# A reordered opening: latents normalised on VectorE, table rows made on GpSimd, third keys ahead of the second half's queries, and expert weights loaded whole

## What is computed

```python
x = x + xattn(layernorm(x), ctx, cos, sin, ...)
x = x + attn(layernorm(x), ...)
x = x + ffn(layernorm(x), ...)
# xattn, b = 8 batches, 16 heads of 64
lat = layer_norm(latents, ln_lat_g, ln_lat_b)
ctx = layer_norm(context, ln_ctx_g, ln_ctx_b)
q = lat @ Wq;  k, v = split(ctx @ Wkv)
k = apply_rope(k, cos, sin)
attn = softmax(clip(q k^T * 64**-0.5, -11, 11));  out = (attn v) @ Wo + bo
# ffn: for the two experts e chosen for a token
out_e = relu(x @ W1[e] + b1[e]) @ W2[e] + b2[e]
```

## Time and profile before

| | |
|---|---|
| median of 3 runs | 1197.59 us (1196.59 to 1199.62) |
| the profiled execution | 1197.26 us, its span 1195.5 us |
| TensorE busy | 1177.0 us (98%) |
| VectorE, ScalarE, GpSimd busy | 1005.6, 649.5, 610.0 us |
| granted TensorE clock | 0.998 over the span |

### The profile page before, as it was taken

How to read it: one execution, slowest core, us unless ns; L and a number is a source line. 1 busy time by engine, 2 the same in 40 slices (tenths; PEclk the granted TensorE clock), 3 DMA queues, 4 the chain that set the end, 5 groups by cost and what they waited for, 6 DMA issues and landing times.

```text
span 1195.5 us, 37336 instructions
## 1 busy us (share of the span) xinstructions
PE 1177.0 (98%) x15252; PEld 992.1 (83%) x15252; DVE 1005.6 (84%) x1923; ACT 649.5 (54%) x1089; POOL 610.0 (51%) x611
## 2 busy tenths in 40 slices
PE   8999999999999999999999999999999999999997
PEld 4787888888888888888888888888888788899997
DVE  7999999999899999999988999998766366768886
ACT  6765555555555555555555555555434243366664
POOL 3576565565655656556666556565452133333333
PEclk9999999999999999999999999999999999999999
DMA  6376665666656665556666566655662721576662
GB/s 239 90 190 155 149 139 145 152 157 161 145 150 151 156 158 145 139 147 151 162 155 151 143 154 155 159 144 121 165 137 72 247 78 58 175 215 207 182 208 57
DMA packets 136180, 181.21 MB, mean 152 GB/s; under 512 B 30332, under 2 KB 96328, under 8 KB 135880
## 3 DMA queue, kind: packets, MB, share of 16 engines
q1 hardware_dynamic: 110552, 150.80, 48.2%
q10 hardware_dynamic: 21376, 23.80, 7.9%
q0 software_dynamic: 4080, 4.22, 1.7%
HBM read 81.93 MB, written 30.56 MB: 94 GB/s over the span
## 4 chain that ended last, share of the span: by engine, by line
PE 89%; DVE 4%; DMA 2%; ACT 2%; issue 1%; SPq 1%; POOL 0%; POOLq 0%; ACTq 0%; DVEq 0%
PE bank L1627 28%; PE bank L1659 28%; PE bank L1600 10%; PE bank L1985 6%; PE bank L1680 3%; PE bank L1789 2%; PE bank L2035 2%; PE bank L2036 2%; PE bank L2037 2%; PE bank L1842 1%; DVE pr L1104 1%; DMA wk_raw<-in_L_xattn_Wkv_dram 1%; PE bank L1885 1%; PE bank L1866 1%; PE bank L1851 1%
## 5 line engine op out<-in xcount | busy, mean ns | idle before, releaser
L1627 PE MATMUL bank<-ct,wk_hi 128*128 128x512 f32 x1024 | 323.5, 397 | 0.7 <-DVE ct L1138 0.7
L1659 PE MATMUL bank<-p_hi,xc 128*128 128x512 f32 x1024 | 316.0, 390 | 0.0
L1659 PEld LDWEIGHTS bank<-p_hi,xc 128*128 128x128 f32 x1024 | 191.8, 188 | 39.7
L1627 PEld LDWEIGHTS bank<-ct,wk_hi 128*128 128x128 f32 x1024 | 187.2, 188 | 41.9 <-issue 1.3
L594 POOL TENSOR_TENSOR kr<-kr,ksw 128x1024 f32<-128x1024 f32 x64 | 153.0, 2391 | 106.9 <-issue 105.5
L1132 DVE TENSOR_TENSOR kw<-bank,stab 128x512 f32<-128x512 f32 x256 | 175.6, 686 | 31.9 <-PE bank L1627 25.3
L1627 PE MATMUL bank<-ct,wk_lo 128*128 128x512 f32 x512 | 200.1, 391 | 0.0
L1659 PE MATMUL bank<-p_lo,xc 128*128 128x512 f32 x512 | 199.2, 389 | 0.0
L790 ACT CAST p_hi<-pr 128x1024 fp32r<-128x1024 f32 x128 | 134.2, 1048 | 89.1 <-DVE pr L1104 88.9
L1104 DVE TENSOR_SCALAR pr<-pr 128x1024 f32<-128x1024 f32 x128 | 137.6, 1075 | 41.5 <-ACT pr L785 39.6
L1120 DVE TENSOR_TENSOR p_lo<-pr,p_hi 128x1024 fp32r<-128x1024 f32 x128 | 168.9, 1320 | 0.5 <-ACT p_hi L790 0.4
(11 more groups left out here) (231 smaller groups left out, 2062.2 us busy)
## 6 DMA issues: line engine op xcount, KB each, us to landing
ksw<-kw SPq DMA_DIRECT2D x512, 128.0 KB, 2.3
x_turned<-xt SPq DMA_DIRECT2D x120, 128.0 KB, 3.3
ct_read<-x_turned SPq DMA_DIRECT2D x30, 512.0 KB, 4.8
w_two<-in_L_ffn_W_dram SPq DMA_DIRECT2D x15, 1024.0 KB, 5.1
raw<-in_ctx_dram ACTq DMA_DIRECT2D x56, 256.0 KB, 3.8
x_slots<-fill ACTq DMA_DIRECT2D x32, 258.0 KB, 3.8
w_all<-in_L_ffn_W_dram SPq DMA_DIRECT2D x4, 2048.0 KB, 17.0
wo<-in_L_ffn_W_dram SPq DMA_DIRECT2D x7, 1024.0 KB, 4.9
```

Source lines behind the costliest of these rows:

```text
L1627: last = pe.matmul(psK[:, a * 512:(a + 1) * 512], l[:, k, w], ct[:, h % 3, r, k], start=(m == 0), stop=(m == len(parts) - 1))
L1659: last = pe.matmul(psZ[c], xc[:, slot_, l, t, cols], r[:, i, :, t], start=(f == 0 and m == 0), stop=(f == 1 and m == len(parts) - 1), skip ...
```

## The change

Six edits to the opening, and one to the loads of the experts. (1) `latent_scale` on GpSimd keeps only the power; VectorE computes the variance term in one instruction and normalises all latent tiles, where ScalarE did tiles 2 to 7. (2) The eight instructions that fill `crep` go from VectorE to GpSimd, and `crep_done` counts each table. (3) `biases` writes four groups of 32 output partitions by 256 columns where it wrote two by 512, and stands ahead of `queries(5, 0)`. (4) TensorE's order: `queries(0, 0)` ahead of `table(0)`, `turn_context(6)` and `(7)` sooner, `keys(2)` and then `keys(3)` ahead of, or between, the other half's queries. (5) ScalarE and VectorE follow that order. (6) SyncE copies the bias row in four pieces. (7) The weights of group 3 are loaded whole where they were loaded in halves, and `first_weights(4)` stands ahead of `rows_in(4)`.

```diff
@@ SyncE
-            sp.wait_ge(bias_done, 1)
-            for i in range(2):
-                sp.dma_start(wv[P - 1:P, KC - 1, i * 512:(i + 1) * 512], bias_rows[HALF * i:HALF * i + 1, :]).then_inc(bias_ld, 16)
+            sp.wait_ge(bias_done, 2)
+            for i in range(4):
+                sp.dma_start(wv[P - 1:P, KC - 1, i * D:(i + 1) * D], bias_rows[HALF * i:HALF * i + 1, :]).then_inc(bias_ld, 16)
...
-            e = expert_of(sp, EARLY)
-            first_weights_of(e, EARLY, 0)
+            first_weights(EARLY)
             sp.wait_ge(group_done, 4)
             sp.wait_ge(scattered, 16 * TOPK * TT)
             for g in range(1, GROUPS):
...
+                if g + WB < GROUPS:
+                    sp.wait_ge(h_ps, FT // 2 * (g + 1))
+                    first_weights(g + WB)
                 if g == 1:
-                    first_weights_of(e, EARLY, 1)
                     sp.wait_ge(ys_done, 2)
                     sp.wait_ge(no_done, 2)
                     rows_in(4)
-                if g + WB < GROUPS:
-                    sp.wait_ge(h_ps, FT // 2 * (g + 1))
-                    first_weights(g + WB)
@@ GpSimd
+            def table_rows(f):
+                for r in range(4):
+                    o = crep[:, f, :, r * HALF:(r + 1) * HALF]
+                    last = pool.tensor_scalar(o, cs_raw[:, f], -1.0 if f == 1 and r % 2 == 1 else 1.0, None, ALU.mult)
+                last.then_inc(crep_done, 1)
             latent_scale(0)
+            pool.wait_ge(cs_ld, 32)
+            table_rows(0)
+            table_rows(1)
@@ ScalarE (order; -/+ whole calls)
-            latents_normalised(2)
-            latents_normalised(3)
...
+            query_weights_high(0)
+            queries(1, 0)
             table(1)
-            queries(1, 0)
+            queries(2, 0)
+            context_high(0)
             key_weights(0)
+            queries(3, 0)
+            context_high(1)
             key_weights(1)
...
+            context_high(6)
+            context_high(7)
             lat_turned(6)
             lat_turned(7)
@@ VectorE
+            latent_variances(0)
+            latents_normalised(0)
...
+            key_weights(1)
             latent_moments(6)
             latent_moments(7)
+            latent_variances(1)
...
+            latents_normalised(1)
             context_low(4)
@@ TensorE
+            queries(0, 0)
             table(0)
-            queries(0, 0)
+            queries(1, 0)
             table(1)
-            queries(1, 0)
             for g in range(2, 7):
+                if g == 5:
+                    biases()
                 queries(g, 0)
                 turn_context(g - 2)
...
+            turn_context(6)
             keys(1)
             turn_lat(6)
             turn_lat(7)
-            biases()
-            turn_context(6)
+            turn_context(7)
             queries(7, 0)
-            turn_context(7)
+            keys(2)
             queries(0, 1)
             queries(1, 1)
-            keys(2)
+            keys(3)
             queries(2, 1)
-            keys(3)
             queries(3, 1)
```

More of the change, by code:

```diff
@@ L114, in build @@
             w_last = sb("w_last", [P, INNER], F32, first)
-            bias_rows = sb("bias_rows", [DH, 512], F32, first)
+            bias_rows = sb("bias_rows", [P, D], F32, first)
+            sb("between_0", [P, D], F32, first)
             crep = sb("crep", [P, 2, ST, P], F32, first)
@@ L721, in lat_turned @@
                 act.wait_ge(latT_ps, t + 1)
-                for k in range(1 if t < TT // 2 else KC):
+                for k in range(1 if 0 < t < TT // 2 else KC):
                     last = act.activation(latT[:, k, t * P:(t + 1) * P], lat_bank(t, k), ACT.Identity,
@@ L732, in biases @@
                 act.wait_ge(bias_ps, 1)
-                act.copy(bias_rows[:], bank[0:DH, 4, :]).then_inc(bias_done, 1)
+                act.copy(bias_rows[:], bank[:, 4, 0:D]).then_inc(bias_done, 1)
             def sum_out(n, c):
@@ L1048, in latent_moments, with latent_variances, latents_normalised @@
                 dve.bn_aggr(xl_mom[:, t], xl_st6[:, t]).then_inc(xl_stats, 1)
+            def latent_variances(c):
+                t = slice(c * TT // 2, (c + 1) * TT // 2)
+                dve.wait_ge(xl_stats, (c + 1) * TT // 2)
+                dve.tensor_scalar(xl_vpe[:, t], xl_mom[:, t, 1], 1.0 + EPS, EPS * EPS, ALU.mult, ALU.add).then_inc(xl_var, 1)
+            def latents_normalised(c):
+                dve.wait_ge(xl_rstd, c + 1)
+                for t in range(c * TT // 2, (c + 1) * TT // 2):
+                    dve.tensor_scalar(xl[:, t], xl[:, t], xl_mom[:, t, 0:1], xl_rsd[:, t:t + 1], ALU.subtract, ALU.mult).then_inc(xl_norm, 1)
             for t in range(TT // 2):
                 latent_moments(t)
[L1052 to L1060, removed]
-                dve.tensor_scalar(xl[:, t], xl[:, t], xl_mom[:, t, 0:1], xl_rsd[:, t:t + 1], ALU.subtract, ALU.mult).then_inc(xl_norm, 1)
+            latent_variances(0)
+            latents_normalised(0)
             dve.wait_ge(vec_done, 1)
-            for u in range(TT // 2):
+            for u in range(1, TT // 2):
                 dve.wait_ge(latT_ps, u + 1)
@@ L1204, in _ @@
             context_low(5)
-            keys_turned(-3, 0)
-            keys_turned(-3, 1)
-            for u in range(TT // 2):
-                latents_low(u)
-            query_weights_low(0)
-            shifts(-3)
-            counted(-3)
-            context_low(6)
             dve.wait_ge(bias_ps, 1)
@@ L1215, in _ @@
             value_weights(0)
-            value_weights(1)
-            context_low(7)
+            keys_turned(-3, 0)
+            keys_turned(-3, 1)
+            context_low(6)
+            shifts(-3)
+            counted(-3)
+            context_low(7)
+            query_weights_low(0)
+            for u in range(TT // 2):
+                latents_low(u)
+            keys_turned(-2, 0)
+            keys_turned(-2, 1)
+            query_weights_low(1)
             blocks_turned(-3)
-            query_weights_low(1)
             shifts(-2)
@@ L1571, in turn_lat @@
             def turn_lat(t):
-                if t < 2:
-                    pe.wait_ge(xl_norm, t + 1)
-                else:
-                    pe.wait_ge(xl_norm_act, t - 1)
+                pe.wait_ge(xl_norm, t + 1)
                 if t == 0:
@@ L1719, in biases @@
                 for k in range(KC):
-                    for c in range(2):
-                        last = pe.matmul(bank[c * HALF:(c + 1) * HALF, 4, :], bcol[:, k], wv[:, k, c * 512:(c + 1) * 512], start=(k == 0), stop=(k == KC - 1))
+                    for c in range(4):
+                        last = pe.matmul(bank[c * HALF:(c + 1) * HALF, 4, 0:D], bcol[:, k], wv[:, k, c * D:(c + 1) * D], start=(k == 0), stop=(k == KC - 1))
                 last.then_inc(bias_ps, 1)
@@ L1754, in _ @@
             pe.wait_ge(ctf_done, ST)
-            pe.wait_ge(bias_done, 1)
+            pe.wait_ge(bias_done, 2)
             scores(1)
@@ L1978, in hidden @@
                 if first == 0:
-                    pe.wait_ge(w1_ld[g % WB], 16 * (g // WB + 1 + (1 if g >= EARLY and g % WB == EARLY % WB else 0)))
+                    pe.wait_ge(w1_ld[g % WB], 16 * (g // WB + 1))
                     pe.wait_ge(xsT_done, g + 1)
```

69 lines of the change are left out of this document (23 added, 46 removed).

## The result

The kernel after takes 1199.91 us (median of 20 runs, 1198.41 to 1204.45) where the kernel before, on the same chips, takes 1197.45 us (20 runs, 1196.19 to 1201.11). The ratio is 1.0018 with a 95% interval of 1.0009 to 1.0026: 2.2 us slower, inside the 0.3% that I called no change. 1198.4 was predicted, 1.5 us under the median, so the loss is twice the 1.1 us of the prediction's sum. The profiled execution has a span of 1198.7 us at a mean granted clock of 0.997.

What follows compares the result with a forecast made beforehand. VectorE's way through the end of the opening was taken to decide, with TensorE 98% busy. 1197.26 + 1.9 (opening) - 0.8 (experts) = 1198.4 us; forecast's own span 1197.0 to 1199.6, all but 2 in 10 within 1195.0 to 1200.6.

Steps and rivals of the forecast that it cites:

- the prediction's sum: Whole kernel: 1197.26 plus 1.9 lost in the opening minus 0.8 gained at the experts gives 1198.4 us.
- The bound: End of the opening: VectorE's progress decides, not TensorE's first scores; a lead of TensorE alone is waited off by 105.
- The start: First queries on TensorE: start at about 10.7 where the table started at 11.22, so TensorE gains 0.5 and VectorE nothing.
- Table rows: Eight rows moved to GpSimd: 0.4 us each, upper bound 0.73, all hidden; VectorE's spared 1.71 us worth nothing.
- Biases: Bias matmuls on TensorE: four groups take 0.95 instead of 1.91, sparing 0.9 us, hence again lead only.
- TensorE's waits: Opening: 1.8 us wait at third keys, first scores near 49.4 (lead 1.5), then about 1.5 each behind two late key sums.
- The holds: VectorE at 44 to 56: GpSimd's key sums hold a value weight 1.2 and a query-weight part 1.5; clamp 1.9 later.
- Experts: Weights of groups 3 and 4: both waits go, 1.5 us, less 0.7 for later rows; gain 0.8, between -0.2 and 1.5.
- forecast of no change: Measured time: a difference within about 0.3% (3.6 us) counts as the same, given chance 0.83.

Runs made afterwards that it cites:

- e3: Kernel after with the second value weight on VectorE moved up ahead of one turned block: 1198.80 us, ratio 1.0005 to before.
- e12: Kernel after with the biases back in two groups of 512 columns and their row copied in two pieces: 1200.43 us, ratio 1.0020 to before.
- e5: Kernel before with GpSimd's first three key sums cut to 64 of 1024 columns: 1197.31 us, ratio 0.9996 to before.
- e10: e9 with one more VectorE instruction at the very start, a memset of an unused column: 1197.02 us, ratio 0.9997 to before.
- e11: Kernel after with the eight table rows back on VectorE: 1200.59 us, ratio 1.0021 to before.
- e6: Kernel after with GpSimd's first three key sums cut to 64 of 1024 columns: 1195.49 us, ratio 0.9976 to before.
- e2: Kernel before with only the expert loads of after: 1196.64 us, ratio 0.9990 to before.
- e8: Kernel after with three moves in VectorE's order (query-weight part, first key turning, eighth context part): 1197.85 us, ratio 1.0000 to before.
- e9: Kernel after with VectorE's order rewritten from the fifth context part to the last query-weight part: 1196.48 us, ratio 0.9990 to before.
- e4: Kernel after with a held query-weight part on VectorE moved behind a shift and counts: 1198.88 us, ratio 1.0008 to before.
- e7: Kernel after with keys of steps 2 and 3 back among TensorE's other-half queries, VectorE's order kept: 1205.10 us, ratio 1.0058 to before.
- e1: Kernel after with the expert loads of before, so the opening alone: 1201.22 us, ratio 1.0030 to before.

## Why the prediction was right, and where it was not

**The bound.** That VectorE's way through the end of the opening sets the first outputs, and not the first scores, held: clamp and outputs moved together (0.97 and 0.97 in e3, 0.76 and 0.79 in e12), and first scores at 49.76 (49.4 told) went with outputs 1.85 late. From the end of the clamp to the outputs it is 48.2 to 48.4 us in 12 of the 14 profiles. The two others, e5 (49.1) and e10 (49.6), are those in which VectorE waited about 3 us or more for turned context (2.94 and 3.46): the way to the outputs is VectorE's and that landing's.

**The start.** Queries at 10.55 for 10.7: right. **Table rows.** Mis-sized: 0.4 was taken, with 0.73 as the upper bound; the trace has 0.83 (6.63 for eight). They ended at 13.88, and GpSimd's variance step for the context, whose statistics stood at 13.2, began only then. Its power was still done at 15.26, as VectorE came to the end of its own statistics at 15.29, so nothing arrived, with next to nothing to spare. e11 shows that they cost nothing. The Trainium skill (GPSIMD Engine Reference, Engine selection) puts two-input elementwise work on GpSimd at about half VectorE's speed and one-input work at roughly line rate. These rows have one input and take four times as long as on VectorE (0.83 against 0.21), and the measurement decides.

**Biases.** The size was right (1.07 for 0.95), its worth wrong: "hence again lead only" is the step that fell. e12 shows 0.8 of the 0.84 arriving at the outputs. Without that edit the opening's loss would have been 2.6 by these single profiles. Why the sum still came out: VectorE's times were carried forward from TensorE's, with the 0.9 in them, and only the sentence on it was false.

**TensorE's waits.** 1.8 was given for the third keys, 1.47 measured (start 38.69 for 38.2); 1.5 each for the two waits behind late sums, 1.16 and 0.87 measured. First scores came 1.16 early, where a lead of 1.5 was told.

**The holds.** Right in kind, place and size: 1.2 and 1.5 us were told for the two, 1.05 and 1.27 measured (e6 against after); 45.3 to 47.7 was told for the value weight, 45.91 to 48.23 measured; the query-weight part from 50.55, held until 52.49 (52.2 told); the clamp at 56.18 (56.2). The total was told as 1.9 at 106.8 and is 1.85 at 106.71. e5 and e6 show that they are the cause of the opening's loss. That the value weight would be held, of which before had no instance, was drawn from its two on-chip inputs; the trace shows 2.32 against 1.28. The Trainium skill (GPSIMD Engine Reference, Specifications) names that pair, and the trace agrees.

**Experts.** The gain was mis-sized, 0.8 for 1.2 in e2 (0.1 to 2.2) and in the trace. 0.7 were charged for later rows, and that wait of 1.0 was placed at group 3: it stands at group 0's rows (1025.40 in before), ahead of the edit. The rows of group 3 cost 0.57 in after.

**What the sum left out.** 1.9 - 1.2 is 0.7, and 2.2 (1.1 to 3.1) was measured. The profile of after shows what came on top. The delay grew by 0.4 at 943, of which a longer wait for a mask product is 0.3, by 0.25 at 1015 and by 0.2 near 1096. With these the sum is 1.5; the prediction had them at nothing. The first is missing in e3, e8, e9 and e11, and what sets the second stays open (e10). The profile of after is 3.2 us longer than that of before, and the rest is the half clock between 1012 and 1036, 1.7 us in the profiles of after, e4, e8 and e12 and 3.4 in e9. The latter isn't peculiar to the new opening. Of the runs with a recorded clock, a mean of 0.997 or less stands in 29 of 102 of before, and in 46 of 119 of the kernels with the new opening (e7 left out; the mean takes in the whole span and doesn't say where the clock fell); the runs of after above 0.997 have a median of 1199.37, the others 1201.18, and those of before (35 runs) 1197.30 and 1200.25. So after is 2.1 us slower above 0.997 and 0.9 at or under it, and whether the new opening brings the fall more often is left open by 28% against 39%. That the forecast of no change came true rests on the 0.3%: the sum of 1.1 us was half of what was measured.

## What to carry to other kernels

Where GpSimd runs long two-input operations, look along the other engine's new order for each two-input or on-chip-to-on-chip operation that comes to lie under one: the price is the rest of GpSimd's operation, not a share. An order that is right for the engine that is 98% busy must be drawn again for the one that follows it; here the same edit on TensorE went with 2.2 us of loss (after) or 1.2 of gain (e9), by VectorE's order alone; the gain is no more than that of the expert loads (e2). And before time spared on the bound engine is called worthless, ask where the other engine waits for it: where two engines wait for each other, it can arrive nearly whole (0.79 of 0.84 us in e12).

## What the runs showed of the hardware

- A VectorE operation with two inputs in on-chip memory outside PSUM, or the clamp, waits out the rest of a GpSimd two-input operation that began before it (2.32 us for 1.27, 1.94 for 0.67, 2.36 for 0.66), while key turning, which reads PSUM, keeps its 0.68. It goes the other way too: in e6 GpSimd's low row, begun at 46.16 under the value weight (45.63 to 46.90), took 1.34 instead of 0.74.
- A one-input GpSimd operation of 128x256, writing rows of 32, takes 0.83 us, more than its two-input one of 128x255 (0.73).
- The granted clock fell to its half level (1.2 of 2.4 GHz) for 3 to 7 us between 1012 and 1036, and in e7 behind gaps of 3.4 and 2.1 us. The gaps of TensorE at 1012 to 1020 don't decide it: after and e1 have it busy 3.50 and then 3.15 of 4 us there, and were granted 0.70 and 1.00 in the second stretch. A mean clock of 0.997 or less stood in some executions of every kernel.
- The same four transfers took SyncE 2.44 us to issue in one profile and 3.70 or 3.88 in others, and turned context landed 5.2 to 7.3 us after its first issue over the profiles, with no change to either.
